# Stack stage: mix by head with 64 key rows, values copied from SBUF to SBUF, centred norms

## The chip, the cores and the metric
One core of a Trainium2 chip runs the whole program. The time is that of the device, from launch to end, in microseconds (us); three runs of the kernel before are given, and one execution that the profiler took.

## The reference
Eight sub-layers in a row work on x, of shape (2, 512, 128): an attention to 77 context rows by dynamic time warping, a quantised feed-forward, two attentions to the context with a mixture of experts between, a stack of six layers, an attention to latents and a second mixture of experts. Ahead of each a norm is taken. The change touches the norms and the stack. A layer of the stack, cut:

```
q, k, v = split(x @ Wqkv)                        # 16 heads of 64
q = rotary(l2norm(q)); k = rotary(l2norm(k))
bk, bv = [previous window of 32, own window]     # 64 keys for 32 queries
attn = softmax(where(mask, -big, 8 * q @ bk.T))
x = x + (attn @ bv) @ Wo
x = x + gelu-gated feed-forward(layernorm(shift(x)))
```
The norms compute `(x - mean) / sqrt(var + eps)`, some with `* gamma + beta`, some applied twice.

## The kernel before
x is kept with its 128 features in the partitions and its 1024 tokens along them, as two halves b of 512. TensorE (PE), VectorE (DVE), ScalarE (ACT), GpSimd (POOL) and SyncE (SP, which issues DMAs) each run a program of their own whose order is written out by hand; they meet only through semaphores.

**Norm.** `Norm.pe` multiplies each half with a matrix of 1/128 (the mean in every row, L174). `dve_centre` subtracts it on DVE (`xc`, L219), ACT squares (L208), PE sums the squares of each token (L186), ACT takes the root, DVE the reciprocal, PE spreads it over the partitions (L193), and DVE multiplies (L232, or L235 and with gamma and beta L237). With `plain` a second product goes to another tile (L241). It is used nine times: ahead of all sub-layers, and once within the third.

**Stack.** Twelve units u (six layers, two halves) of four tiles of 128 tokens make 48 tiles T. In round T of the loop PE projects tile T+2 (`pe_proj`, L1401: values in m = 0 and 1, then queries and keys), transposes r of T+1 (L1509), computes scores (L1530), transposed probabilities (L1582) and the mix (L1602) of T, and transposed output (L1626) and output product (L1650) of T-1. The feed-forward of unit u lies in the first two tiles of the unit after: its norm in t = 0, its products (L1740, L1742, L1765) in t = 1. t = 2 and 3 are plain tiles. PE may start projection m when the bank is free: the last two wait for `qk_used`, which DVE signals after its second table product (st_t, L1444).

Two heads e lie in one pair c: e = 0 in partitions 0 to 63, e = 1 in 64 to 127, each with 32 keys of the previous window (h = 0) and 32 of the own (h = 1). The scores are 64 products per tile, one for each pair, window w and head. The mix is 32 per tile: the stationary st_pT holds both heads in 128 rows and 32 queries, the moving st_vv 128 columns: for each head 64 columns, with zeros in the other head's rows. Each fp32 product makes two weight loads and two matmuls in the trace.

The values reach st_vv by way of DRAM: `sp_shift(T)` stores st_v (512 KB, L1343) when ACT has evacuated it, waits until mix T-2 is done, loads the last window of T-1 (only for t > 0), waits for the store, and loads four (256 KB) and three (192 KB) windows for each head (L1333). st_v and st_vv have two buffers. ACT overwrites st_v of tile T-2 once `v_stored` says that it is in DRAM (L1412). The loads of the next layer's weights are issued on SP behind tiles t = 3 to 6 of each layer (L1311 to L1323).

Of the kernel before, what the change touches and what calls it, by code (L numbers as in the profile page):

```python
# [78 lines left out]
def build(nc, io):  # L79
# [66 lines left out]
    class Norm:  # L146
# [3 lines left out]
        def __init__(self, tag, parts=(0, 1), chain=None):  # L150
            self.parts, self.chain = parts, chain or order
            self.mean_ready = sem(tag + "_mean_ready")
# [16 lines left out]
        PLAIN = (5, 4)  # L169

        def pe_mean(self, pe, b, src, src_ready, banks):
            if src_ready is not None:
                pe.wait_ge(src_ready, n("pe", src_ready))
            pe.matmul(PS[:, banks[b], :], const("mean"), src[:, b, :], start=True, stop=True)\  # L174
              .then_inc(self.mean_ready, 1)

        def pe(self, pe, src, src_ready, plain=False, banks=(6, 7), made=0):
# [4 lines left out]
            for b in self.parts:  # L182
                pe.wait_ge(self.squared, n("pe", self.squared))
                for j in range(self.BLOCKS):
                    at = self.BLOCKS * b + j
                    mm = pe.matmul(PS[:, banks[self.parts[0]], at:at + 1], sq[:, b, P * j:P * j + P],  # L186
                                   const("mean")[:, 0:1], start=True, stop=True)
# [15 lines left out]
        def act(self, act, twice=False, banks=(6, 7)):  # L203
# [6 lines left out]
            var = PS[:, banks[self.parts[0]], 0:B * self.BLOCKS]  # L210
# [10 lines left out]
        def dve(self, dve, src, dst, gamma=None, beta=None, twice=False, plain=None, banks=(6, 7), made=0):  # L221
            self.uses["dve"] = self.uses.get("dve", 0) + 1
            c = self.chain
            for b in self.parts[made:]:
                self.dve_centre(dve, b, src, banks)
# [3 lines left out]
            for b in self.parts:  # L229
# [18 lines left out]
    class Align:  # L248
# [151 lines left out]
        def ctx_pe(self, pe):  # L400
            pe.matmul(PS[:, 6, 0:B * KC], const("mean"), ctxT[:, :], start=True, stop=True).then_inc(norm.mean_ready, 1)
# [9 lines left out]
        def ctx_dve(self, dve):  # L411
            dve.wait_ge(norm.mean_ready, n("dve", norm.mean_ready))
            order.link(dve, dve.tensor_tensor(self.c0[:, :], ctxT[:, :], PS[:, 6, 0:B * KC], ALU.subtract))
            dve.tensor_tensor(self.c1[:, :], self.c0[:, :], self.c0[:, :], ALU.mult).then_inc(norm.squared, 1)

# [510 lines left out]
    class PairAttention:  # L926
# [41 lines left out]
        def act(self, act):  # L968
# [10 lines left out]
            norm.act(act)  # L979

        def dve(self, dve):
# [22 lines left out]
            norm.dve(dve, self.h2, xn, column("pa_ln2w"), column("pa_ln2b"))  # L1004
# [217 lines left out]
    class Stack:  # L1222
# [13 lines left out]
        def __init__(self):  # L1236
# [24 lines left out]
            self.v_out = dram("st_v_out", (4, P, INNER))  # L1261

            self.vv = s("vv", [P, 8, 2, INNER // 2])
# [15 lines left out]
             self.sub_done, self.exps, self.den_ready, self.rden_ready, self.v_stored, self.pv_done, self.on_ready,  # L1279
# [6 lines left out]
                "sub_done exps den_ready rden_ready v_stored pv_done on_ready wo_done xu_ready xf_ready centred lnsq "  # L1286
                "var std rstd spread ln_tmp ffn_in up gelu act_ready down down_added scaled masked").split()]
            self.vshift = [sem("st_vshift%d" % t) for t in range(4)]

# [38 lines left out]
        def v_load(self, sp, T, e, h, first, count, to, signal):  # L1328

            rows = slice(64 * e + WIN * h, 64 * e + WIN * h + WIN)  # L1330
            src = view(self.v_out, ((T % 4) * P + WIN * first) * INNER + 512 * e,
                       [[INNER, WIN], [WIN * INNER, count], [1, 512]])
            sp.dma_start(self.vv[rows, to:to + count, e, :], src).then_inc(self.vshift[signal], 16)  # L1333

        def sp_shift(self, sp, T):

            t = T % self.TILES
            at = 4 * (T % 2)
# [65 lines left out]
        def act_proj(self, act, T, m):  # L1404
# [189 lines left out]
        def pe_mix(self, pe, T):  # L1594
# [3 lines left out]
            pe.wait_ge(self.vshift[t], (u + 1) * (64 if t == 0 else 96))  # L1598
            for c in range(8):
                for w in range(4):  # L1600
                    g = slice(WIN * w, WIN * w + WIN)
                    mm = pe.matmul(PS[g, c // 4, P * (c % 4):P * (c % 4) + P], self.pT[:, c, g],  # L1602
                                   self.vv[:, 4 * (T % 2) + w, :, D2 * c:D2 * c + D2], start=(c % 4 == 0), stop=(c % 4 == 3),
                                   tile_position=(0, WIN * w), skip_group_check=True)
            mm.then_inc(self.pv_done, 1)

        def dve_out(self, dve, T):
            dve.wait_ge(self.pv_done, T + 1)
            dve.wait_ge(self.rden_ready, T + 1)
            if T > 0:  # L1610
                dve.wait_ge(self.o_turned, 2 * T)
            dve.tensor_tensor(self.on[:, :, :, :].rearrange("p (b c) e d -> p b (c e) d", b=2),
                              PS[:, 0:2, :].rearrange("p b (h d) -> p b h d", h=8),
                              self.rden[:, T % 2, :].rearrange("p (b h) -> p b h", b=2).unsqueeze(3)
# [281 lines left out]
        def dve(self, dve):  # L1896
# [7 lines left out]
            for T in range(-2, self.N + 3):  # L1904
# [34 lines left out]
                if end_of == self.LAST:  # L1939
                    norm.dve_centre(dve, 0, x, latents.NORM_BANKS)  # L1940
                    latents.ctx_dve(dve)

        def pool(self, pool):

            for k, what in enumerate((self.xs[64:P, :, 0:1], self.xf[64:P, 0:1], self.kT[:, :, 0:WIN],
                                      self.vv[:, 0:4, :, :], self.vv[:, 4:8, :, :])):
# [430 lines left out]
    def _(act):  # L2377
# [7 lines left out]
        norm.act(act, twice=True)  # L2385
# [7 lines left out]
        norm.act(act, twice=True, banks=latents.NORM_BANKS)  # L2393
        latents.act(act)
        norm.act(act, twice=True)
# [25 lines left out]
    def _(dve):  # L2421
        align.strips_dve(dve)
        dve.wait_ge(loaded, 16 * LOADS)
        norm.dve(dve, x, xn)
        align.dve(dve)
        norm.dve(dve, x, xn)
        quantised.dve(dve)
        norm.dve(dve, x, xn)
        attend1.dve(dve)
        norm.dve(dve, x, xn, column("pa_ln1w"), column("pa_ln1b"), twice=True, plain=pair.h0)  # L2430
        pair.dve(dve)
        experts1.dve(dve, pair.h2)
        norm.dve(dve, x, xn)
        attend2.dve(dve)
        norm.dve(dve, x, stack.y0)
        stack.dve(dve)
        norm.dve(dve, x, xn, column("la_g2"), column("la_b2"), twice=True,
                 banks=latents.NORM_BANKS, made=1)
        latents.dve(dve)
        norm.dve(dve, x, xn, column("m3_g"), column("m3_b"), twice=True, plain=h7)  # L2440
# [7 lines left out]
def spans(parts):  # L2448
    at, out = 0, {}
    for name, width in parts:  # L2450
# [6 lines left out]
                     ("hm", H), ("kidx", E), ("threehalves", 1), ("iota", S), ("blk8", P), ("centre", P)])  # L2457
# [113 lines left out]
```

## Time and profile before
| | us |
|---|---|
| median of 3 runs | 1928.72 (1924.58 to 1930.95) |
| the profiled execution | 1930.89 |
| its span, first to last instruction | 1929.1 |
| PE, DVE, ACT, POOL busy | 1614.8, 1254.7, 985.0, 760.8 |
| mean granted clock of TensorE | 0.92 of full speed |

Matmuls (PE) and weight loads (PEld) are shown as two engines. An arrow "<-DVE st_t L1444" behind a row names what ended the idle time before it; "issue" is idle time that nothing in the profile ended. A granted clock of 1.00 is TensorE's upper level, 2.4 GHz, and 0.50 its lower, 1.2 GHz.

### The profile page before, as it was taken

The numbers are of one execution on the slowest core, as the hardware profiler recorded it, in microseconds if no ns is written. First come the engines' busy times: TensorE is split into PE (matmuls) and PEld (weight loads), VectorE is DVE, ScalarE is ACT, GpSimd is POOL, SyncE is SP. The second block draws the span as 40 slices with busy tenths as digits, with TensorE's granted clock in tenths as the row PEclk, the third lists the DMA queues.
The fourth block names the chain that finished last, engine by engine and source line by source line (L and its number), as shares of the span: only waits on it lengthen the run. The fifth ranks groups of instructions, "written<-read, shape, count | busy, mean of one in ns | idle before, by whom it ended". The sixth has DMA issues, their size and how long they took to land. (4 is left out here: it accounts for less than half of the span.)

```text
span 1929.1 us, 42065 instructions
## 1 busy us (share of the span) xinstructions
PE 1614.8 (84%) x17121; PEld 1094.3 (57%) x17121; DVE 1254.7 (65%) x2359; ACT 985.0 (51%) x1853; POOL 760.8 (39%) x1082
## 2 busy tenths in 40 slices
PE   3005576998777899999999889999888999999999
PEld 1002264675645566666666666666664677666676
DVE  6847694213956788878887778888863666666311
ACT  1034133332335567657666556666654776777232
POOL 0000030100366576766776667776740333333000
PEclk6556698999979999999999999999998999999899
DMA  3000002010043433523533434433230000000111
GB/s 109 20 4 0 3 1 62 23 33 14 1 132 91 111 96 104 150 64 103 141 90 99 108 87 113 112 105 89 86 90 1 1 1 1 1 1 1 34 33 33
DMA packets 73801, 113.35 MB, mean 59 GB/s; under 512 B 16082, under 2 KB 36152, under 8 KB 73578
## 3 DMA queue, kind: packets, MB, share of 16 engines
q1 hardware_dynamic: 72794, 110.42, 20.7%
q8 instruction: 137, 2.24, 0.5%
q14 instruction: 54, 0.44, 0.1%
q10 hardware_dynamic: 816, 0.24, 0.1%
HBM read 83.96 MB, written 27.50 MB: 58 GB/s over the span
## 5 line engine op out<-in xcount | busy, mean ns | idle before, releaser
L1478 POOL TENSOR_TENSOR st_r<-st_r,st_t 128x512 f32<-128x512 f32 x192 | 243.8, 1274 | 212.0 <-DVE st_t L1444 212.0
L1401 PE MATMUL PS<-st_wqkv,st_xs 128*128 128x512 f32 x576 | 306.0, 616 | 12.2 <-DVE st_t L1444 7.7
L2252 POOL TENSOR_SCALAR la_p<-la_p,la_rden 128x589 f32<-128x589 f32 x64 | 112.9, 1763 | 232.9 <-DVE la_rden L2271 232.9
L1495 POOL TENSOR_TENSOR st_r<-st_r,st_gy 128x512 f32<-128x512 f32 x192 | 195.1, 1049 | 3.8
L1436 DVE TENSOR_TENSOR st_r<-PS,st_rot 128x512 f32<-128x512 f32 x192 | 129.2, 673 | 99.8 <-ACT st_sqh L1420 99.2
L1188 ACT ACTIVATE m_h<-PS 128x512 f32<-128x512 f32 x128 | 76.5, 598 | 143.0 <-PE PS L1120 143.0
L2265 DVE TENSOR_REDUCE la_nmx<-PS 128x1 f32<-128x589 f32 x128 | 92.7, 766 | 84.8 <-PE PS L2110 84.8
L1420 ACT ACTIVATE st_sqh<-PS 128x512 f32<-128x512 f32 x192 | 114.5, 597 | 57.6 <-PE PS L1401 57.0
L2217 ACT ACTIVATE la_p<-PS,la_nmx 128x589 f32<-128x589 f32 x128 | 95.2, 748 | 82.0 <-DVE la_nmx L2265 81.9
L1213 DVE SCALAR_TENSOR_TENSOR m_y<-PS,m_g,m_y 128x128 f32<-128x128 f32 x112 | 31.5, 344 | 161.0 <-PE PS L1129 161.0
L803 POOL MEMSET l_s<- 128x144 f32 x2 | 0.4, 220 | 331.7 <-DVE x L645 217.6
L1129 PEld LDWEIGHTS PS<-m_w,m_h 128*128 128x128 f32 x1024 | 121.4, 196 | 16.0 <-issue 16.0
L1444 DVE TENSOR_TENSOR st_t<-PS,st_rot 128x512 f32<-128x512 f32 x192 | 130.3, 679 | 0.0
L1449 DVE TENSOR_REDUCE st_ss<-st_sqh 128x8 f32<-128x512 f32 x192 | 129.5, 675 | 0.0
L1509 PEld LDWEIGHTS PS<-cst,st_r 128*128 128x128 f32 x768 | 91.2, 144 | 62.7 <-issue 44.4
L1129 PE MATMUL PS<-m_w,m_h 128*128 128x128 f32 x1024 | 121.6, 279 | 3.0 <-DVE m_y L1215 3.0
L1120 PE MATMUL PS<-xn,m_w 128*128 128x512 f32 x256 | 118.9, 610 | 0.0
L1650 PEld LDWEIGHTS PS<-st_oT,st_wo 128*128 128x128 f32 x768 | 94.4, 199 | 38.8 <-ACT st_oT L1635 29.1
L1509 PE MATMUL PS<-cst,st_r 128*128 128x128 f32 x768 | 111.1, 278 | 4.5 <-POOL st_r L1495 3.7
L1650 PE MATMUL PS<-st_oT,st_wo 128*128 128x128 f32 x768 | 102.1, 288 | 4.8 <-issue 2.7
L1401 PEld LDWEIGHTS PS<-st_wqkv,st_xs 128*128 128x128 f32 x576 | 89.7, 195 | 26.7 <-DVE st_t L1444 16.2
L1530 PE MATMUL PS<-st_kT,st_qT 64*32 64x64 f32 x6144 | 73.8, 226 | 36.1 <-issue 27.5
(312 smaller groups left out, 3483.2 us busy)
## 6 DMA issues: line engine op xcount, KB each, us to landing
st_v_out<-st_v SPq DMA_DIRECT2D x48, 512.0 KB, 2.6
st_vv<-st_v_out SPq DMA_DIRECT2D x96, 256.0 KB, 3.8
st_vv<-st_v_out SPq DMA_DIRECT2D x96, 192.0 KB, 4.4
st_wqkv<-in_st_wqkv SPq DMA_DIRECT2D x18, 512.0 KB, 5.8
m_w<-in_m_w SPq DMA_DIRECT2D x32, 256.0 KB, 3.2
st_vv<-st_v_out SPq DMA_DIRECT2D x72, 64.0 KB, 1.9
st_wo<-in_st_wo SPq DMA_DIRECT2D x6, 512.0 KB
st_w<-in_st_w SPq DMA_DIRECT2D x6, 341.0 KB
```

The source lines that it names most:

```text
L1120: pe.matmul(PS[:, c, :], self.w1[:, e % 2, P * c:P * c + P], xn[:, b, :], start=True, stop=True)\
L1129: mm = pe.matmul(PS[:, 4 + u % 2, P * j:P * j + P], self.h[:, u % 2, c, P * j:P * j + P], self.w2[:, e % 2, c, :], start=(c == 0), stop=(c ...
L1401: pe.matmul(PS[:, 2 + m % 2, :], self.xs[:, b, P * t:P * t + P], self.wqkv[:, l % 2, k, 512 * half:512 * half + 512], start=True, stop=Tru ...
L1420: act.activation(self.sqh[:, c % 2, :], ps, ACT.Square).then_inc(self.squares, 1)
L1436: dve.tensor_tensor(h3(self.r[:, t % 2, c, :]), h3(ps), self.rot[:, k, 0, t, :].unsqueeze(1) .broadcast_to([P, 8, D2]), ALU.mult)
L1444: dve.tensor_tensor(h4(self.t2[:, c % 2, :]), turned, self.rot[:, k, 1, t, :] .rearrange("p (s d) -> p s d", s=2).unsqueeze(1).broadcast_t ...
L1449: dve.tensor_reduce(self.ss[:, t % 2, 8 * c:8 * c + 8], h3(self.sqh[:, c % 2, :]), X, ALU.add)\
L1478: pool.tensor_tensor(r, r, self.t2[:, c % 2, :], ALU.add).then_inc(self.added, 1)
L1495: pool.tensor_tensor(r, r, y[:, 8 * c:8 * c + 8].unsqueeze(2).broadcast_to([P, 8, D2]), ALU.mult)\
L1509: mm = pe.transpose(PS[:, 4 + g % 2, P * j:P * j + P], self.r[:, T % 2, g, P * j:P * j + P], ident)
L1650: mm = pe.matmul(PS[:, 7, 0:P], self.wo[:, l % 2, c, :], self.oT[:, c, :], start=(c == 0), stop=(c == 7))
L2252: pool.tensor_scalar(self.p[:, v % 2, 0, :], self.p[:, v % 2, 0, :], self.rden[:, v % 4, 0:1], None, ALU.mult).then_inc(self.scaled0, 1)
```

## The change
**Mix.** 64 products per tile, one for each pair, window and head, with 64 stationary rows and 64 moving columns. st_vv loses its zeros: 512 columns per window instead of 1024. The result of head e goes to bank e of PSUM, and `dve_out` reads it in that order.

**Values.** No DRAM. `sp_shift(T)` waits for the evacuation and for mix T-2, and issues 14 DMAs from st_v to st_vv, of 32 rows by 2 KB each, preceded for t > 0 by two that cross from tile T-1. These two signal on semaphores of their own, `v_crossed`. ACT waits for the copies of T-2 and for the crossing copies of T-1 before it overwrites st_v, the mix for both kinds.

**Norms.** PE multiplies with `centre` (identity less 1/128), so the product is centred. ACT squares it from PSUM; DVE copies it to xc once it is squared. The variance goes to bank 5. With gamma, DVE does one scalar_tensor_tensor and ACT adds beta. `centre` moves into the first load of constants. At the stack's end `dve_keep` stands where `dve_centre` stood.

```diff
         def pe_mean(self, pe, b, src, src_ready, banks):
-            pe.matmul(PS[:, banks[b], :], const("mean"), src[:, b, :], start=True, stop=True)\
-              .then_inc(self.mean_ready, 1)
+            pe.matmul(PS[:, banks[b], :], const("centre"), src[:, b, :], start=True, stop=True)\
+              .then_inc(self.centred, 1)
...
-                act.activation(sq[:, b, :], xc[:, b, :], ACT.Square).then_inc(self.squared, 1)
+                act.activation(sq[:, b, :], PS[:, banks[b], :], ACT.Square).then_inc(self.squared, 1)
...
+            for b in self.parts if beta is not None else ():
+                act.wait_ge(self.scaled, n("act", self.scaled))
+                act.activation(dst[:, b, :], dst[:, b, :], ACT.Identity, bias=beta).then_inc(self.normed, 1)
-        def dve_centre(self, dve, b, src, banks):
-            dve.wait_ge(self.mean_ready, n("dve", self.mean_ready))
-            dve.tensor_tensor(xc[:, b, :], src[:, b, :], PS[:, banks[b], :], ALU.subtract).then_inc(self.centred, 1)
+        def dve_keep(self, dve, b, banks):
+            dve.wait_ge(self.squared, n("dve", self.squared))
+            dve.tensor_copy(xc[:, b, :], PS[:, banks[b], :])
...
-                    c.link(dve, dve.tensor_tensor(dst[:, b, :], xc[:, b, :], PS[:, banks[b], :],
-                                                  ALU.mult))
-                    dve.tensor_scalar(dst[:, b, :], dst[:, b, :], gamma, beta, ALU.mult, ALU.add)\
-                       .then_inc(self.normed, 1)
+                    dve.scalar_tensor_tensor(dst[:, b, :], xc[:, b, :], gamma, PS[:, banks[b], :], ALU.mult, ALU.mult)\
+                       .then_inc(self.scaled, 1)
...
+        def v_copy(self, sp, T, e, h, w, signal):
+            source = 4 * T + w - (1 - h)
+            rows = slice(64 * e + WIN * h, 64 * e + WIN * h + WIN)
+            block = slice(WIN * (source % 4), WIN * (source % 4) + WIN)
+            sp.dma_start(self.vv[rows, 4 * (T % 2) + w, :],
+                         self.v[block, source // 4 % 2, 512 * e:512 * e + 512]).then_inc(signal, 16)
...
         def sp_shift(self, sp, T):
             sp.wait_ge(self.v_evac, T * 2 + 2)
-            if T >= 4:
-                sp.wait_ge(self.pv_done, T - 3)
-            sp.dma_start(self.v_out[t], self.v[:, t % 2, :]).then_inc(self.v_stored, 16)
             if T >= 2:
                 sp.wait_ge(self.pv_done, T - 1)
             if t > 0:
                 for e in range(2):
-                    self.v_load(sp, T - 1, e, 0, 3, 1, at, t)
-            sp.wait_ge(self.v_stored, T * 16 + 16)
+                    self.v_copy(sp, T, e, 0, 0, self.v_crossed[T % 2])
             for e in range(2):
-                self.v_load(sp, T, e, 1, 0, 4, at, t)
-                self.v_load(sp, T, e, 0, 0, 3, at + 1, t)
+                for w in range(4):
+                    self.v_copy(sp, T, e, 1, w, self.vshift[t])
+                    if w:
+                        self.v_copy(sp, T, e, 0, w, self.vshift[t])
...
-                    act.wait_ge(self.v_stored, T * 16 - 16)
+                    act.wait_ge(self.vshift[(T - 2) % self.TILES], ((T - 2) // self.TILES + 1) * self.OWN)
+                    act.wait_ge(*self.crossed(T - 1))
...
             for c in range(8):
                 for w in range(4):
-                    mm = pe.matmul(PS[g, c // 4, P * (c % 4):P * (c % 4) + P], self.pT[:, c, g],
-                                   self.vv[:, 4 * (T % 2) + w, :, D2 * c:D2 * c + D2], start=(c % 4 == 0), stop=(c % 4 == 3),
-                                   tile_position=(0, WIN * w), skip_group_check=True)
+                    for e in range(2):
+                        keys = slice(64 * e, 64 * e + 64)
+                        mm = pe.matmul(PS[g, e, D2 * c:D2 * c + D2], self.pT[keys, c, g],
+                                       self.vv[keys, 4 * (T % 2) + w, D2 * c:D2 * c + D2], start=(c == 0), stop=(c == 7),
+                                       tile_position=(64 * e, WIN * w), skip_group_check=True)
...
                 if end_of == self.LAST:
-                    norm.dve_centre(dve, 0, x, latents.NORM_BANKS)
+                    norm.dve_keep(dve, 0, latents.NORM_BANKS)
                     latents.ctx_dve(dve)
```

## Rows read from the trace of the kernel before
**Rows 1.** Stretches: busy us (instructions) of PE, PEld, DVE, ACT, POOL; PEclk, DMA share, GB/s.
```profile
551.00:1452.00 901.00, 828.67 (x12452) 553.98 (x12452) 702.14 (x1083) 566.53 (x925) 597.19 (x984) 0.98 0.37 103
736.00:806.00 70.00, 68.26 (x1049) 45.49 (x1044) 58.61 (x92) 47.58 (x79) 48.38 (x82) 1.00 0.41 115
```

**Rows 2.** Timeline, PE (start us, us, engine, line): first parts of two mixes.
```profile
735.58 1.63 PE L1602 MATMUL PS<-st_vv,st_pT 128*32 128x128 f32 x52
805.55 1.72 PE L1602 MATMUL PS<-st_vv,st_pT 128*32 128x128 f32 x54
```

**Rows 3.** Waits of PE's matmuls in the stack: total us, times, longest.
```profile
PE PS L1530 <- issue: 27.5, 10, 4.4
PE PS L1626 <- issue: 6.1, 2, 3.4
...
PE PS L1740 <- DVE st_hid L1757: 3.8, 6, 0.6
...
PE PS L1650 <- issue: 2.7, 2, 2.1
```

**Rows 4.** Timeline, PE: one scores block, cut in two.
```profile
610.27 1.37 PE L1530 MATMUL PS<-st_kT,st_qT 64*32 64x64 f32 x116 [1.26 <-ACT PS L1545]
616.06 0.46 PE L1530 MATMUL PS<-st_kT,st_qT 64*32 64x64 f32 x12 [4.42 <-issue]
```

**Rows 5.** The page: busy time; the code queue; a DMA group (count, KB, landing).
```profile
PE 1614.8 (84%) x17121; PEld 1094.3 (57%) x17121; DVE 1254.7 (65%) x2359; ACT 985.0 (51%) x1853; POOL 760.8 (39%) x1082
...
q8 instruction: 137, 2.24, 0.5%
...
st_vv<-st_v_out SPq DMA_DIRECT2D x72, 64.0 KB, 1.9
```

**Rows 6.** Stretches (columns as rows 1): before and in that stall.
```profile
608.00:613.00 5.00, 2.38 (x122) 1.74 (x120) 4.67 (x9) 2.48 (x4) 2.71 (x3) 0.93 1.03 256
614.00:617.00 3.00, 0.94 (x13) 0.71 (x14) 0.40 (x1) 0.00 (x0) 2.30 (x10) 0.50 0.00 0
```

**Rows 7.** Timeline of a quiet plain tile: DVE, PE, ACT and SP.
```profile
919.82 0.69 DVE L1436 TENSOR_TENSOR st_r<-PS,st_rot 128x512 f32<-128x512 f32 x1 [1.21 <-ACT st_sqh L1420]
...
921.25 1.95 PE L1602 MATMUL PS<-st_vv,st_pT 128*32 128x128 f32 x64
923.14 0.66 PE L1509 MATMUL PS<-cst,st_r 128*128 128x128 f32 x4
...
927.23 1.12 PE L1401 MATMUL PS<-st_wqkv,st_xs 128*128 128x512 f32 x2 [0.40 <-DVE st_t L1444]
928.28 1.48 PE L1530 MATMUL PS<-st_kT,st_qT 64*32 64x64 f32 x128
928.39 0.60 ACT L1413 ACTIVATE st_v<-PS 128x512 f32<-128x512 f32 x1
929.69 0.66 PE L1626 MATMUL PS<-cst,st_on 128*128 128x128 f32 x4
...
934.62 0.69 DVE L1436 TENSOR_TENSOR st_r<-PS,st_rot 128x512 f32<-128x512 f32 x1 [1.20 <-ACT st_sqh L1420]
...
938.43 2.68 SPq L1333 DMA_DIRECT2D st_vv<-st_v_out  x6
```

**Rows 8.** SBUF to SBUF DMAs of the alignment: issue ns (min/median/max), busy share.
```profile
L311 SPq DMA_DIRECT2D al_skew<-al_dist x8: 774/775/955, 20.3 to 26.2; - x8
...
20.00:29.00 9.00, 2.96 (x15) 1.63 (x13) 7.70 (x13) 0.81 (x2) 0.00 (x0) 0.79 0.21 34
```

**Rows 9.** Norms: the second half ahead of the stack, and two operations by line.
```profile
541.80 0.69 DVE L219 TENSOR_TENSOR xc<-x,PS 128x512 f32<-128x512 f32 x1 [0.42 <-PE PS L174]
...
542.52 0.63 ACT L208 ACTIVATE sq<-xc 128x512 f32<-128x512 f32 x1 [0.48 <-DVE xc L219]
...
L237 DVE TENSOR_SCALAR xn<-xn,vec x8: 545/546/547, 301.4 to 1804.4; 128x512 f32<-128x512 f32 x8
...
L922 DVE SCALAR_TENSOR_TENSOR x<-PS,vec,x x4: 743/747/751, 287.8 to 539.8; 128x512 f32<-128x512 f32 x4
```

More of the change, by code:

```diff
@@ L146, in build, with __init__ @@
     class Norm:
-        def __init__(self, tag, parts=(0, 1), chain=None):
-            self.parts, self.chain = parts, chain or order
-            self.mean_ready = sem(tag + "_mean_ready")
+        def __init__(self, tag, parts=(0, 1)):
+            self.parts = parts
+            self.scaled = sem(tag + "_scaled")
             self.centred = sem(tag + "_centred")
@@ L185, in pe @@
                     at = self.BLOCKS * b + j
-                    mm = pe.matmul(PS[:, banks[self.parts[0]], at:at + 1], sq[:, b, P * j:P * j + P],
+                    mm = pe.matmul(PS[:, self.VAR, at:at + 1], sq[:, b, P * j:P * j + P],
                                    const("mean")[:, 0:1], start=True, stop=True)
@@ L201, in pe, with act @@
                 mm.then_inc(self.spread_ready, 1)
-        def act(self, act, twice=False, banks=(6, 7)):
+        def act(self, act, twice=False, beta=None, dst=None, banks=(6, 7)):
             self.uses["act"] = self.uses.get("act", 0) + 1
@@ L215, in act, with dve @@
                 act.activation(rstd[:, 0, :], var, ACT.Sqrt, bias=const("eps")).then_inc(self.std_ready, 1)
-        def dve_centre(self, dve, b, src, banks):
-            dve.wait_ge(self.mean_ready, n("dve", self.mean_ready))
-            dve.tensor_tensor(xc[:, b, :], src[:, b, :], PS[:, banks[b], :], ALU.subtract).then_inc(self.centred, 1)
-        def dve(self, dve, src, dst, gamma=None, beta=None, twice=False, plain=None, banks=(6, 7), made=0):
+            for b in self.parts if beta is not None else ():
[4 more added lines that the diff above has]
+            dve.tensor_copy(xc[:, b, :], PS[:, banks[b], :])
+        def dve(self, dve, dst, gamma=None, twice=False, plain=None, banks=(6, 7), made=0):
             self.uses["dve"] = self.uses.get("dve", 0) + 1
-            c = self.chain
             for b in self.parts[made:]:
-                self.dve_centre(dve, b, src, banks)
+                self.dve_keep(dve, b, banks)
             dve.wait_ge(self.std_ready, n("dve", self.std_ready))
@@ L400, in ctx_pe @@
         def ctx_pe(self, pe):
-            pe.matmul(PS[:, 6, 0:B * KC], const("mean"), ctxT[:, :], start=True, stop=True).then_inc(norm.mean_ready, 1)
+            pe.matmul(PS[:, 6, 0:B * KC], const("mean"), ctxT[:, :], start=True, stop=True).then_inc(self.prod_ready, 1)
             pe.wait_ge(norm.squared, n("pe", norm.squared))
@@ L411, in ctx_dve @@
         def ctx_dve(self, dve):
-            dve.wait_ge(norm.mean_ready, n("dve", norm.mean_ready))
+            dve.wait_ge(self.prod_ready, B + 1)
             order.link(dve, dve.tensor_tensor(self.c0[:, :], ctxT[:, :], PS[:, 6, 0:B * KC], ALU.subtract))
             dve.tensor_tensor(self.c1[:, :], self.c0[:, :], self.c0[:, :], ALU.mult).then_inc(norm.squared, 1)
+            n("dve", norm.squared)
         def ctx_out_dve(self, dve):
@@ L978, in act @@
                .then_inc(self.exps, 1)
-            norm.act(act)
+            norm.act(act, beta=column("pa_ln2b"), dst=xn)
         def dve(self, dve):
@@ L1003, in dve @@
             dve.wait_ge(self.h2_ready, 2)
-            norm.dve(dve, self.h2, xn, column("pa_ln2w"), column("pa_ln2b"))
+            norm.dve(dve, xn, column("pa_ln2w"))
     class Experts:
@@ L2384, in _ @@
         attend1.act(act)
-        norm.act(act, twice=True)
+        norm.act(act, twice=True, beta=column("pa_ln1b"), dst=xn)
         attend2.kv_act(act, 3)
@@ L2392, in _ @@
         stack.act(act)
-        norm.act(act, twice=True, banks=latents.NORM_BANKS)
+        norm.act(act, twice=True, beta=column("la_b2"), dst=xn, banks=latents.NORM_BANKS)
         latents.act(act)
-        norm.act(act, twice=True)
+        norm.act(act, twice=True, beta=column("m3_b"), dst=xn)
         experts3.act(act)
@@ L2423, in _ @@
         dve.wait_ge(loaded, 16 * LOADS)
-        norm.dve(dve, x, xn)
+        norm.dve(dve, xn)
         align.dve(dve)
-        norm.dve(dve, x, xn)
+        norm.dve(dve, xn)
         quantised.dve(dve)
-        norm.dve(dve, x, xn)
+        norm.dve(dve, xn)
         attend1.dve(dve)
-        norm.dve(dve, x, xn, column("pa_ln1w"), column("pa_ln1b"), twice=True, plain=pair.h0)
+        norm.dve(dve, xn, column("pa_ln1w"), twice=True, plain=pair.h0)
         pair.dve(dve)
         experts1.dve(dve, pair.h2)
-        norm.dve(dve, x, xn)
+        norm.dve(dve, xn)
         attend2.dve(dve)
-        norm.dve(dve, x, stack.y0)
+        norm.dve(dve, stack.y0)
         stack.dve(dve)
-        norm.dve(dve, x, xn, column("la_g2"), column("la_b2"), twice=True,
+        norm.dve(dve, xn, column("la_g2"), twice=True,
                  banks=latents.NORM_BANKS, made=1)
         latents.dve(dve)
-        norm.dve(dve, x, xn, column("m3_g"), column("m3_b"), twice=True, plain=h7)
+        norm.dve(dve, xn, column("m3_g"), twice=True, plain=h7)
         dve.wait_ge(norm.plain_ready, 4)
```

36 lines of the change are left out of this document (20 added, 16 removed).

## The prediction
> **What bounds the kernel now.** I read the busy time by stage first. The stack stage is 901 of the 1929.1 us. TensorE is busy for 92% of it, VectorE for 78%, and the mix lies in it 48 times [rows 1]. The starts of the mix give the period [rows 2]: 735.58 and 805.55 with three between, so four quiet tiles take 69.97 us. Twelve such fours would be 840 us; filling and emptying the pipeline takes part of the rest of the 901, and another part is lost within.
>
> The list of waits says where: TensorE stands for 27.5 + 6.1 + 2.7 = 36.3 us in 14 waits that no semaphore ends ("issue"), ten of them before the scores [rows 3]. In the order of time one is seen to cut a scores block in two: 116 matmuls, nothing for 4.42 us, then the last 12 [rows 4]. Nothing in the program separates the 116th from the 117th. What does is code. The instruction queue q8 moved 137 packets of 16 KB [rows 5]; TensorE's 2 x 17,121 matmuls and weight loads make 250 instructions for each, some more with its waits. And a stall goes with full DMA engines: from 608 to 613 their busy share was 1.03, from 614 it was 0.00, and TensorE went on at 616.06 [rows 4, 6]. The code block stood behind data packets, and once these were gone it took about 3 us to arrive and to take effect. Behind the stall TensorE's clock is at its lower level, 1.2 GHz (granted clock 0.50 in 614 to 617, rows 6).
>
> Then one quiet tile, to see what the mix is worth [rows 7]. From 919.82 VectorE works without a break past 927.17, where its table product lets TensorE start a projection, for which TensorE had waited 0.40 us. TensorE then works through scores, transposes, the output product and a projection; ScalarE squares it, and VectorE, idle for 1.20 us, goes on at 934.62. That loop of 14.80 us is the tile. The mix (921.25) lies beside its VectorE half, and the wait of 0.40 us behind the mix is slack of TensorE.
>
> **The mix.** Before: 64 matmul records from 921.25 to the next instruction at 923.14, 1.89 us. After: 64 products of 64 rows, 32 columns and 64 moving columns, in 128 records: in form, count and order the scores, 928.28 to 929.69, 1.41 us [rows 7]. 0.48 us less in 48 tiles is 23.0 us if all of it counted. In a plain tile it doesn't: TensorE comes 0.48 earlier to the projection for which it already waits 0.40. In the tile with the end of the feed-forward it waits for VectorE right after the mix too (L1740 behind st_hid, 0.6 us [rows 3]). Only in the tile with the norm, and in tiles that stalls have made TensorE's, some of it is kept. I take 4 us (12 norm tiles at 0.2, the rest from disturbed ones); ends 0 and 23. What a change of tile shape costs lies in these intervals, with neighbours of the full shape in either kernel.
>
> The Trainium skill (TensorEngine Tiling (Array Packing), section Instruction Overhead) says that a matmul costs some 60 cycles whatever its length, and that row tiling gives up to twice the speed. This case has a row for the very form, 1.41 and not 0.95 us, so the row is used; with 0.95 the upper end of the saving would be 45 us, an estimate by that page.
>
> **Code.** The mix doubles its instructions: 64 more matmuls and 64 more weight loads in each of 48 tiles, 6144, or 24 code blocks more. Today a tile holds one run that eats 256 instructions in 1.41 us (scores), and one of 128 in 1.89. After it holds two of 256 in 1.41. A block that lies inside such a run is used up before the next can come, and TensorE stands. So twice as many places can stall: 28 for today's 14. But the stalls will be shorter. Today's mean is 2.6 us because the loads of st_vv and of weights fill the DMA engines for some five us after a mix (share 1.03 at 608 to 613 [rows 6]). After, SP feeds that queue slowly (below), and the block comes when it is asked for: of the 3 us a part is covered by what TensorE still has, I take 1.2 us each, 34 us. Half of them lie around the mix, where TensorE has 0.40 + 0.48 us of slack: 14 x 0.88 = 12 us less, leaves 22. And fewer are long enough to bring the clock down. Against 36.3: 14 us gained, with 1 taken off for weight loads, 13. Ends: 28 stalls as long as today's, 73 us, a loss of 36; 14 of 1.2, 17, a gain of 19.
>
> **The copies of the values.** Removed per tile: the store of st_v (512 KB), the wait for it, and four to six loads (six in 2.68 us [rows 7], 0.45 each). Added: 14 copies, 16 in tiles with a predecessor, of 64 KB each, from SBUF to SBUF. SP took 0.775 us for one such DMA at the alignment [rows 8], against 0.45 for one from DRAM: 16 x 0.775 = 12.4 us per tile, ends 7.2 (at 0.45) and 15.3 (at 0.955, the longest there). With a weight load it is 12.9, under the plain tile's 14.8. So SP hides it. Queued behind are the weight loads of the next layer, some 10 us later; they have whole tiles to come. 32 packets per 0.775 us are 2 for each of 16 engines. Today SP puts the same 1024 KB (2 x 256, 2 x 192, 2 x 64) into the queue within 2.68 us [rows 7]: that is why the engines were full.
>
> The new wait is ScalarE's before it overwrites st_v: it needs the crossing copies, the first two that SP issues after the mix. Mix ends 923.14, SP issues at 923.27, two issues take 1.55, a landing 1.9 (the 64 KB load, rows 5): 926.7. ScalarE wants them at 928.39 [rows 7], 1.7 us later. Behind it queue the transposed output and the second value copy; they could bear another us, as the projection that needs the bank comes four us later. I cost it at nothing; were each landing 3 us longer, 1 us in 36 tiles, 36 us. The memset of st_vv on GpSimd halves; VectorE's own work ahead of the stack hides it: 0 (nothing lost if not).
>
> **The norms.** Nine of them. Today: product, VectorE centres (541.80, 0.69 us), ScalarE squares (542.52) [rows 9]. After: ScalarE reads the centred product from PSUM when VectorE would have, and the square is 0.72 us earlier. VectorE's copy to xc (under 0.7 each) lies beside the variance's 16 matmuls and the root. All nine stand between stages on the chain: 9 x 0.72 = 6.5. Four have a gamma: today 0.69 (a product as L219) + 0.546 (L237) per half, one after the other on VectorE; after 0.747 (the form of L922) and 0.63 on ScalarE (as its square) beside the next half [rows 9]. The first half comes 0.14 later, the second at 2.12 instead of 2.47, with the wait between dropped some 0.4 earlier; together 1.0. Costs: the first load of constants grows by 64 KB, 0.3 us at 256 GB/s [rows 6]. At the stack's end the copy must wait for ScalarE's square, which stands behind a gelu and a table load, and VectorE's last addition of the stack waits behind it; today there is idle time ahead of that addition: 0.2, at most 2. Sum 7.0; ends 3 and 11.
>
> **Sum.** On the profiled execution's 1930.89 (span 1929.1 and 1.8 around it): -7 -4 -13 = 1906.9. The median of the runs is 2.2 lower, so 1904.7: **1905 us**.
>
> **Rivals.**
> - *The whole of the mix counts.* For it: TensorE is busy for 97% of a quiet stretch (68.26 of 70 us, rows 1). Against: the 0.40 us wait and the loop above. 1928.7 -7 -23 -13 = 1886.
> - *The stalls stay what they are*, more but shorter in equal measure, or not of code at all; the mix brings 2. 1928.7 -7 -2 = 1920. The Trainium skill (Runtime: NRT & Kernel Launch, section Instruction fetch mechanics) leads here: it puts 256 instructions in a block of 16 KB, which the 137 packets agree with, but says that fetching is mostly hidden. The cut scores blocks speak against that.
> - *Slower: the code comes late.* Every block waits behind copies as today, and there are twice the short blocks. Place: inside scores and mix; price 36 us; it decides if a 2 KB packet between SBUF and SBUF takes over 0.39 us (two in 0.775), for then the engines are full all the time. Against: at the alignment such DMAs back to back gave a busy share of 0.21 [rows 8]. 1928.7 -7 -4 +36 = 1954.
> - *Slower: SP becomes the bound*, over (14.8 - 0.45) / 16 = 0.90 us per copy. At 1.1 us, 18.1 in the 24 plain tiles, 3.3 each: 79 us, 1984.
>
> **Chances.** Forecast 0.45 (own range 1896 to 1914), whole mix 0.13, stalls stay 0.22, code late 0.14, SP 0.06. Under 0.3% (5.8 us) a measurement can't tell from no change. Faster by more: 0.45 + 0.13 + two thirds of 0.22, 0.72. Within: 0.11. Slower: 0.17. The range leaves out the late code, most of SP and a tail of the first rival: 1884 to 1932.
>
> **What would show it.** Right: st_pT's matmuls as 128 records in 1.4 us; the projection's wait for st_t near 0.9 us in plain tiles, and the period of four quiet tiles at 69 to 70 us; DMA share never near 1 for 5 us outside weight loads; issue waits more in number, near or under 1.5 us; norm squares straight behind L174. Wrong: a quiet four under 68.5 us (mix counts), issue waits summing to over 40 us, SP's copies back to back into the next mix, or ScalarE idle before L1413 for a DMA.

## The result: slower by 0.6%, where 1.2% faster was forecast
| | median us (lowest to highest) | runs |
|---|---|---|
| before | 1929.01 (1918.31 to 1938.19) | 20 |
| after | 1941.58 (1924.46 to 1950.58) | 20 |

The ratio of after to before is 1.0062, 95% interval 1.0041 to 1.0082. In a later comparison it was 1.0038 (1.0012 to 1.0065). I had forecast 1905, with a range of 1884 to 1932: the time lies outside, on the side of the rival "the code comes late".

The profiled execution of after took 1928.86 us (span 1927.0), the low end of its runs; a second one, taken beside the last experiments, took 1943.39 (span 1941.6). Where they differ I give both. The page of the first, busy time and code queue:

```profile
span 1927.0 us, 48632 instructions
...
PE 1594.3 (83%) x20193; PEld 1077.1 (56%) x20193; DVE 1254.0 (65%) x2351; ACT 991.1 (51%) x1861; POOL 756.0 (39%) x1082
...
q8 instruction: 161, 2.64, 0.6%
```

Against [rows 5] there are 3072 more matmuls, as many more weight loads, and 161 code blocks for 137: the 24 more that I had counted. TensorE's busy time has fallen by 20 us. The mix itself became as quick as reckoned. The timeline of TensorE, mixes of some quiet tiles:

```profile
1041.62 1.49 PE L1618 MATMUL PS<-st_vv,st_pT 64*32 64x64 f32 x128
...
1061.64 1.49 PE L1618 MATMUL PS<-st_vv,st_pT 64*32 64x64 f32 x128
...
1076.80 1.48 PE L1618 MATMUL PS<-st_vv,st_pT 64*32 64x64 f32 x128
...
1267.31 1.49 PE L1618 MATMUL PS<-st_vv,st_pT 64*32 64x64 f32 x128
...
1318.30 1.48 PE L1618 MATMUL PS<-st_vv,st_pT 64*32 64x64 f32 x128
...
1335.91 1.33 PE L1618 MATMUL PS<-st_vv,st_pT 64*32 64x64 f32 x111
```

Tiles without a stall, against those of before: t = 1 took 20.02 us (1041.62 to 1061.64; 21.14 before), t = 2 15.16 (15.16), t = 3 15.87 to 16.03 (15.66). t = 0 took 17.61 once (1318.30 to 1335.91), but 18.2 to 18.5 in three others (18.01). Four quiet tiles are 68.6 us where four lie in a row (1267.31 to 1335.91), and 69.3 to 69.7 when added up with the other values of t = 0: 0.3 to 1.4 less than before [rows 2]. If tiles stayed quiet, the kernel would be faster. They don't. The waits of TensorE's matmuls by line (us in total, times, longest), first execution, and then the lines of the second:

```profile
PE PS L1542 <- issue: 31.1, 16, 2.8
...
PE PS L1618 <- issue: 15.2, 12, 1.7
...
PE PS L1642 <- issue: 3.8, 2, 2.1
```
```profile
PE PS L1542 <- issue: 32.5, 15, 2.9
PE PS L1618 <- issue: 17.0, 13, 1.8
PE PS L1642 <- issue: 3.7, 2, 2.5
PE PS L1521 <- issue: 2.1, 3, 1.4
PE PS L1666 <- issue: 1.2, 3, 0.5
```

Before, 14 such waits took 36.3 us and none lay in the mix [rows 3]. Now 31 to 34 take 51 to 56, and a dozen cut the mix. One plain tile (t = 3) shows both kinds. The timeline of TensorE:

```profile
921.92 1.28 PE L1618 MATMUL PS<-st_vv,st_pT 64*32 64x64 f32 x105
924.62 0.42 PE L1618 MATMUL PS<-st_vv,st_pT 64*32 64x64 f32 x23 [1.41 <-issue]
...
929.92 1.03 PE L1542 MATMUL PS<-st_kT,st_qT 64*32 64x64 f32 x81 [0.29 <-ACT PS L1557]
933.74 0.84 PE L1542 MATMUL PS<-st_kT,st_qT 64*32 64x64 f32 x47 [2.79 <-issue]
934.51 1.12 PE L1642 MATMUL PS<-cst,st_on 128*128 128x128 f32 x4
935.42 1.92 PE L1412 MATMUL PS<-st_wqkv,st_xs 128*128 128x512 f32 x2
```

The tile lasts 21.07 us instead of 16.0: 4.2 of standing still, and then matmuls at half speed (the projection of two takes 1.92 us, elsewhere 1.02). The stretches of this tile say what the DMA engines did (columns as in rows 1):

```profile
834.00:839.00 5.00, 4.29 (x22) 2.39 (x20) 4.97 (x9) 4.11 (x7) 2.58 (x3) 1.00 0.31 76
...
921.00:926.00 5.00, 3.59 (x140) 2.69 (x139) 4.96 (x8) 1.80 (x4) 5.00 (x6) 1.00 0.06 20
931.00:934.00 3.00, 0.26 (x29) 0.26 (x33) 0.80 (x2) 0.00 (x0) 2.20 (x8) 0.98 0.32 78
934.00:937.00 3.00, 3.00 (x49) 1.90 (x30) 2.34 (x2) 0.60 (x1) 2.53 (x8) 0.50 0.39 93
```

The first row is a quiet tile, behind its mix: a DMA share of 0.31, where before it was 1.03 [rows 6]. Around the stall in the mix the share is 0.06, in the stall of the scores 0.32. The engines are far from full, and TensorE stands all the same: what is left as the cause is a block used up before the next is there. In the 3 us before a stall the share was 0.02 to 0.04 in eight of eleven mixes, and 0.3 to 0.5 before the scores, where the copies were running. Behind the second stall the granted clock is 0.50, the lower level.

**Where the stalls begin.** I numbered TensorE's rows in the trace (matmuls, weight loads and semaphore waits) in order of time, from 0. Of the waits without a releaser above 0.5 us in the stack, all (14 of before, 29 of after) begin at a row whose number is 193 modulo 256: the edge of a code block, not a place of the program. And a packet of q8, which had taken 0.9 to 1.6 us, had ended 1.2 to 1.6 us before TensorE went on.

**An account of the stack** (from its first mix to its last), worked out from each trace: length, stalls at such edges, time at the lower clock level, and the rest, which is length less stalls less half of that time (half, as matmuls take twice as long at the lower level: 1.92 us against 1.02 above). The number counts short stalls too.

| kernel | length | stalls (number) | at half clock | rest |
|---|---|---|---|---|
| before | 858.7 | 36.3 (14) | 30.7 | 807.1 |
| after, first | 873.4 | 50.9 (31) | 41.0 | 802.0 |
| after, second | 881.8 | 55.9 (34) | 51.2 | 800.3 |
| n_only | 857.3 | 31.0 (13) | 38.6 | 807.0 |
| c_only | 838.7 | 16.9 (10) | 17.1 | 813.3 |
| nc | 846.3 | 19.8 (11) | 24.9 | 814.1 |
| m_only | 898.2 | 70.7 (34) | 75.1 | 790.0 |
| nc_split | 890.8 | 51.3 (34) | 52.2 | 813.4 |
| a_wide | 836.0 | 22.6 (15) | 13.7 | 806.6 |
| a_pad224 | 884.6 | 59.7 (38) | 44.4 | 802.7 |
| a_pad96 | 882.1 | 61.0 (38) | 34.1 | 804.0 |
| a_mid | 865.1 | 22.6 (16) | 13.7 | 835.7 |
| a_midp | 875.0 | 35.6 (29) | 14.4 | 832.2 |
| nc_mid | 850.0 | 13.3 (11) | 4.5 | 834.5 |

In the eleven profiles with the order of work unchanged the rest is 790 to 814, while the length ranges over 62 us. Some of the time at half clock lies within the stalls and is counted twice (5.0 us in before, 2.0 and 2.7 in after, 11.2 in m_only), which moves a rest by 6 us at most. How much slow clock goes with how much stall isn't fixed: 51.2 us with 55.9, but 34.1 with 61.0 (a_pad96).

### The profile page after: what moved, and what is told of

The parts are those of the page before. It is cut to its first block and busy times, and to the rows that moved or that the text cites. A ratio compares the mean times of both kernels' runs of the same rounds, so it can differ in the third digit from the quotient of the medians.

```text
span 1927.0 us, 48632 instructions
## 1 busy us (share of the span) xinstructions
PE 1594.3 (83%) x20193; PEld 1077.1 (56%) x20193; DVE 1254.0 (65%) x2351; ACT 991.1 (51%) x1861; POOL 756.0 (39%) x1082
## 5 line engine op out<-in xcount | busy, mean ns | idle before, releaser
L1666 PEld LDWEIGHTS PS<-st_oT,st_wo 128*128 128x128 f32 x768 | 99.3, 207 | 37.3 <-ACT st_oT L1651 28.2
L1542 PE MATMUL PS<-st_kT,st_qT 64*32 64x64 f32 x6144 | 82.7, 227 | 40.0 <-issue 31.1
L1542 PEld LDWEIGHTS PS<-st_kT,st_qT 64*32 64x32 f32 x6144 | 70.9, 106 | 73.7 <-issue 72.2
```

The costliest lines, as they stand in the source:

```text
L1542: mm = pe.matmul(PS[WIN * w:WIN * w + WIN, e, D2 * c:D2 * c + D2], self.qT[64 * e:64 * e + 64, c, WIN * w:WIN * w + WIN], self.kT[64 * e:6 ...
L1666: mm = pe.matmul(PS[:, 7, 0:P], self.wo[:, l % 2, c, :], self.oT[:, c, :], start=(c == 0), stop=(c == 7))
```

## The experiments
Eleven more kernels, and after once more, in 5 to 12 runs each. A ratio is to the kernel before, run on the same chip, and can differ a little from the ratio of the medians.

**The three parts, one at a time.** n_only has the new norms and the stack of before; c_only the new `sp_shift`, with st_vv's zeros and the 32-product mix kept; m_only the new mix, fed by way of DRAM.

```diff
# c_only, in the stack of after (with the mix of before)
-            sp.dma_start(self.vv[rows, 4 * (T % 2) + w, :],
+            sp.dma_start(self.vv[rows, 4 * (T % 2) + w, e, :],
# m_only, in the stack of before
-            sp.dma_start(self.vv[rows, to:to + count, e, :], src)
+            sp.dma_start(self.vv[rows, to:to + count, :], src)
```

n_only. Expected: 

> The kernel before with the new norms alone. If the norms do what was worked out, 7 us less than before (1922), and the stack as before: about 14 issue waits of TensorE, 36 us. If the loss sits in the norms (a wait of VectorE at the stack's end, or ScalarE's extra work), 1929 or more.

c_only. Expected: 

> The kernel before with the direct value copies alone; st_vv keeps its zeros and the mix its 32 products. By the theory that TensorE waits for code behind DMA packets, the issue waits shrink from 36 us, as the DMA engines are no longer full behind each mix: 1905 to 1920. By the rival that 16 small SBUF to SBUF copies per tile cost time (SP, or code late behind them), 1935 to 1945 with as many or longer issue waits.

m_only. Expected: 

> The kernel before with the mix by head alone (64 products, no zeros), values still by way of DRAM. By the theory that the doubled instructions stall for code: 25 to 30 issue waits, as long as today's (2 to 3 us), 1945 to 1965. By the rival that the copies are what costs, the mix alone gives 1915 to 1929.

| | median us | ratio (95%) |
|---|---|---|
| n_only | 1920.65 | 0.9954 (0.9923 to 0.9985) |
| c_only | 1909.77 | 0.9915 (0.9887 to 0.9943) |
| m_only | 1966.17 | 1.0207 (1.0178 to 1.0236) |

The median of before beside them was 1927.65: -7, -18 and +39 us. The waits of c_only, and then of m_only:

```profile
PE PS L1539 <- issue: 14.0, 8, 2.6
PE PS L1637 <- issue: 2.6, 2, 1.8
...
```
```profile
PE PS L1530 <- issue: 44.3, 17, 4.5
PE PS L1604 <- issue: 16.9, 13, 1.7
PE PS L1628 <- issue: 8.7, 2, 4.9
```

The loss is the mix's alone. m_only is the rival "the code comes late" as I had described it, full queue and twice the short blocks: 34 stalls of 70.7 us at the edges. In one of them the DMA engines are full and then TensorE stands at the lower clock:

```profile
600.00:605.00 5.00, 2.83 (x124) 1.93 (x122) 4.86 (x9) 2.82 (x5) 3.08 (x3) 0.98 1.04 236
605.00:608.00 3.00, 0.00 (x0) 0.00 (x0) 0.00 (x0) 0.00 (x0) 2.28 (x10) 0.50 0.31 117
```

In c_only, with the code of before and no burst of copies, stalls last 1.7 us each instead of 2.6, and four of 14 are gone.

Full engines make a stall longer, but it doesn't need them. TensorE's rows are the same, in the same order, in m_only and after, so the same edge can be read in both. At the edge ahead of which m_only's engines were full (600 to 605, above), it stalls 4.46 us and after 2.40; either has 12 matmuls cut off, as in [rows 4]. At an edge where m_only's engines moved nothing, it still stalls 2.45 us, against 2.72 in after. The timeline of m_only and its stretch, then the same edge in after:

```profile
1058.58 0.77 PE L1530 MATMUL PS<-st_kT,st_qT 64*32 64x64 f32 x39 [2.45 <-issue]
1056.00:1058.50 2.50, 0.13 (x15) 0.00 (x0) 0.86 (x2) 1.37 (x4) 1.85 (x6) 1.00 0.00 0
```
```profile
1031.42 0.65 PE L1542 MATMUL PS<-st_kT,st_qT 64*32 64x64 f32 x39 [2.72 <-issue]
```

**Norms and copies without the mix.** nc is after with the zeros and the 32-product mix of before.

Expected: 

> Norms and direct copies with the mix of before: the change without the doubled instructions. By the code theory the best of the four, 1900 to 1912. By the rival that the copies cost, 1930 or more.

Measured: 1905.16 us, ratio 0.9911 (0.9876 to 0.9946). It beats both kernels. To after's ratio of 1.0062 (1.0038) the mix by head adds 0.0151 (0.0127), or 24 to 29 us.

**Is it the number of instructions or the form of the mix?** The mix by head changes both: twice the records, and tiles of 64 rows into banks by head. nc_split has the number without the form, a_wide the form without the number.

```diff
# nc_split: nc, each product in two
-                    mm = pe.matmul(PS[g, c // 4, P * (c % 4):P * (c % 4) + P], self.pT[:, c, g],
-                                   self.vv[:, 4 * (T % 2) + w, :, D2 * c:D2 * c + D2], ...)
+                    for e in range(2):
+                        at = P * (c % 4) + D2 * e
+                        mm = pe.matmul(PS[g, c // 4, at:at + D2], self.pT[:, c, g],
+                                       self.vv[:, 4 * (T % 2) + w, e, D2 * c:D2 * c + D2], ...)
...
# a_wide: after, 128 moving columns
-            for c in range(8):
+            for c in range(0, 8, 2):
...
-                        mm = pe.matmul(PS[g, e, D2 * c:D2 * c + D2], self.pT[keys, c, g],
+                        mm = pe.matmul(PS[g, e, D2 * c:D2 * c + 2 * D2], self.pT[keys, c, g],
...
```

nc_split. Expected: 

> The kernel with the new norms and the direct copies, its values still with zeros beside them and its mix over all 128 rows, but each of the mix's 32 products cut into two of 64 moving columns: 64 products, 128 records, the count of the kernel after, without its head-by-head tiles. The uncut one was 1905 us (ratio to before 0.991). If the doubled count of instructions is what costs, through blocks of code that come late: stalls as in the kernel after (about 30 in the stack, some 45 to 50 us, against 17 to 20 uncut), time 1930 to 1945, ratio 1.00 to 1.01. If it is the form (tiles of 64 rows, banks by head), the time stays at 1900 to 1910.

a_wide. Expected: 

> The kernel after, with its mix by head over 64 key rows, but in 32 products of 128 moving columns instead of 64 of 64 (the second half of the columns gets the weights of the first head: another result, the same form of tile). It has the records of the mix before, 64. If the count of instructions costs: 1900 to 1912 us, ratio near 0.991, issue waits under 25 us in the stack. If the form costs: 1935 to 1945, ratio near 1.006.

Measured: nc_split 1949.02 us, 1.0111 (1.0091 to 1.0130); a_wide 1894.73 us, 0.9827 (0.9803 to 0.9852). The waits of nc_split (its mix is L1618, too) and of a_wide:

```profile
PE PS L1542 <- issue: 34.1, 16, 3.0
PE PS L1618 <- issue: 11.1, 13, 1.4
...
```
```profile
PE PS L1542 <- issue: 20.9, 13, 2.7
PE PS L1642 <- issue: 1.7, 2, 0.9
```

That decides it. With the old form and the doubled number the stalls are there, in the mix as well, and 0.020 of the ratio to nc, 39 us, are lost, more than expected; with the new form and the old number none is in the mix, and it is 0.0084, 16 us, under nc, also more than expected. (Its mix takes 1.16 us, so that some of the 16 is work saved.) It is the number. The mix of nc_split takes 0.6 us longer than that of after, 2.07 us, and its stalls are shorter, 11.1 us in 13 against 15.2 in 12 and 17.0 in 13: what TensorE still has to do covers a part.

**Does it matter where the edges fall?** Waits that are long fulfilled, in an idle time of TensorE's before the stack, push all later edges on.

```diff
# a_pad224, a_pad96 (96 waits): align.pe
             quantised.weights_pe(pe)
+            for _ in range(224):
+                pe.wait_ge(self.xsq, B)
             pe.wait_ge(self.walked, 3)
```

a_pad224. Expected: 

> The kernel after, and nothing else than 224 waits on a semaphore that has long reached its value, executed by TensorE in an idle time of some 50 us during the alignment. They move every later boundary between blocks of 256 instructions by 224 (that is, 32 the other way). In the kernel after every long stall begins at such a boundary, and it stalls where the boundary lies in the last 90 or so instructions of a run of 256 quick ones (scores, mix). Going through the after trace with its stalls taken out and 3.95 us from the entry of one block to the readiness of the next, I get 24 us of stalls unmoved (49 were measured), 15 for this shift. Theory of code: stalls fall to some 32 us, time 1920 to 1930, ratio near 0.998. If the place of code does not matter, 1941, ratio 1.006.

a_pad96. Expected: 

> The same with 96 waits. The same reckoning gives 29 us of stalls where it gives 24 unmoved. Theory of code: stalls near 60 us, time 1945 to 1958, ratio 1.009 to 1.015, and in any case 15 us or more above the version with 224. If the place of code does not matter, 1941, the same as with 224.

Measured: 1945.92 us, 1.0118 (1.0095 to 1.0142), and 1948.44 us, 1.0099 (1.0068 to 1.0131). My numbers missed, and the experiment isn't the one described: two waits went into one instruction, so that the edges moved by 112 and 48 (48744 and 48680 instructions on the pages, against 48632). For these shifts the same reckoning gives some 26 and 18 to 20 us of stalls, where it gives 19 to 24 unmoved, depending on which small gaps are taken out; the traces have 59.7 and 61.0, where unmoved ones have 50.9 and 55.9. It predicts neither the sums nor their order. What the two do show is that the stalls move with the edges: counted with the added rows, 35 waits above 0.5 us of each lie at 193 modulo 256 again, now 112 or 48 instructions earlier in the work.

The place of an edge tells whether it stalls. In the eleven profiles with the order of work unchanged, 418 edges lie in the first 140 rows of a run of 256 quick ones (scores, or the mix of 128 records), and none of them stalls. From row 205 of such a run on, 110 of 111 stall in the six profiles with the long mix (for 0.2 to 4.5 us), and 43 of 55 in the five with the short one. Between, it varies. Of 125 edges in a mix of 64 records, a run of 128 rows, none stalls. So the mix by head made places to stall out of places that had none. How much a given place costs I can't tell in advance.

**Are the stalls shorter where the run of quick instructions is broken?** a_mid moves four transposes into the middle of the scores and four into that of the mix; a_midp a projection into the scores; nc_mid is nc with the first of these. after_again is the kernel after, beside them.

```diff
# a_mid (nc_mid: the scores alone)
             for c in range(8):
+                if c == 4:
+                    between()        # scores: turn_o(T - 1, 0), mix: turn_r(T + 1, 0)
                 for w in range(4):
# a_midp: between() in the scores is pe_proj(T + 2, 0)
```

after_again. Expected: 

> The kernel after once more, beside the two kernels below that rearrange it, and for a second profile of it: the first profiled execution, 1929 us, was at the low end of its runs (median 1942). In the profiles of eight kernels so far the stack, from the first mix to the last, is 802 to 814 us and the sum of the stalls at boundaries of code blocks and half of the time at half clock. Expected 1941 again, ratio 1.006; stalls in the stack 50 to 62 us.

a_mid. Expected: 

> The kernel after with the same instructions, two of them moved: the four transposes of the first half of the output, until now ahead of the scores, stand between the scores of heads 7 and 8, and the four of the first query half, ahead of the mix, stand between the mix of heads 7 and 8. A run of 256 quick instructions becomes two of 128 with 8 slower ones between, and the last block takes 0.6 us longer to use up. If the stalls come because 256 instructions are used up before the next block is there, each is some 0.6 us shorter: 31 x 0.6 = 18 us of stalls and a third of the time at half clock, 1941 becomes 1912 to 1926. If the length of a stall is set by something else (a fixed cost of a boundary), 1938 to 1945. A loss is possible where the later transposes hold up ScalarE: up to 0.6 us in 24 plain tiles.

a_midp. Expected: 

> The kernel after with the first projection of the tile after next (0.9 to 1.0 us), until now ahead of the scores, between the scores of heads 7 and 8; the mix as it was. Theory of code: 18 stalls at the scores shorter by 0.9, 16 us and some clock; but the projection comes 0.7 us later to ScalarE and VectorE, which wait for it in the plain tiles' loop, up to 0.7 x 36 = 25 us lost. 1920 to 1950, stalls at the scores 31 us down to 15 to 20; that sum, not the time, is what tells. Rival: the sum stays at 31.

nc_mid. Expected: 

> The best legitimate kernel so far (new norms and direct copies, the mix of before, 1905 us, ratio 0.991), with the transposes of the first output half between the scores of heads 7 and 8. Theory of code: 10 stalls of the scores shorter by 0.6, 6 us and some clock: 1896 to 1903, ratio 0.985 to 0.990. Rival: 1905.

| | median us | ratio (95%) |
|---|---|---|
| after_again | 1938.39 | 1.0038 (1.0012 to 1.0065) |
| a_mid | 1927.78 | 1.0013 (0.9985 to 1.0042) |
| a_midp | 1939.25 | 1.0051 (1.0030 to 1.0072) |
| nc_mid | 1911.10 | 0.9917 (0.9887 to 0.9947) |

The waits of a_mid, and its timeline (TensorE) around a scores block:

```profile
PE PS L1544 <- issue: 18.9, 12, 2.3
...
PE PS L1622 <- issue: 0.6, 1, 0.6
```
```profile
842.91 1.13 PE L1412 MATMUL PS<-st_wqkv,st_xs 128*128 128x512 f32 x2 [1.05 <-DVE st_t L1456]
843.97 0.86 PE L1544 MATMUL PS<-st_kT,st_qT 64*32 64x64 f32 x64
844.76 0.66 PE L1646 MATMUL PS<-cst,st_on 128*128 128x128 f32 x4
845.34 0.86 PE L1544 MATMUL PS<-st_kT,st_qT 64*32 64x64 f32 x64
```

With the same instructions, 8 slow ones (0.6 us) between two times 128 quick ones cut the stalls from 55.9 to 22.6 us, more than the 18 expected; those of the mix (17.0) all but vanish (0.6), and the low clock goes from 51.2 us to 13.7. The time gains little, 11 us by the medians and 5 by the ratios, whose intervals overlap (expected were 15 to 29), as the rest of the stack is 35 us longer: what was moved is late for its reader, TensorE now waits 1.05 us instead of 0.54 for st_t, and a plain tile takes 15.6 us. (What these longer waits ahead of the scores add to the shorter stalls behind them isn't separated from the break itself.) a_midp shows the same for the scores alone (stalls before them from 32.5 to 18.3 us, nothing gained in time), and in nc, with few stalls to shorten, the move loses about what it brings (0.9917 against 0.9911; 0.985 to 0.990 was expected).

## Why the prediction was wrong
**Norms, -7 (3 to 11): right.** n_only: -7.0 us by the medians, 3 to 15 less by the interval of the ratio. In the timeline of after, around the norm ahead of the stack:

```profile
528.58 2.13 PE L175 MATMUL PS<-x,cst 128*128 128x512 f32 x4
...
529.64 0.60 ACT L209 ACTIVATE sq<-PS 128x512 f32<-128x512 f32 x1 [0.62 <-PE PS L175]
...
530.75 0.60 ACT L209 ACTIVATE sq<-PS 128x512 f32<-128x512 f32 x1 [0.52 <-PE PS L175]
531.38 0.69 DVE L224 COPY xc<-PS 128x512 f32<-128x512 f32 x1 [0.42 <-ACT sq L209]
```

The last square ends 2.77 us after the first product starts, before 3.52 (542.52 + 0.63 less 539.63): 0.75 per norm, reckoned 0.72. The copy lies beside the variance's matmuls.

**Copies cost nothing: right for SP and ScalarE; the sum of their gain came out by luck.** SP issues 14 in 9.96 us, 0.71 each (estimate 0.775), and a landing takes 2.0 us (1.9). ScalarE overwrites st_v without a wait for a DMA; what it waited for here was the projection:

```profile
833.92 9.96 SPq L1342 DMA_DIRECT2D st_vv<-st_v  x14
...
839.55 0.60 ACT L1425 ACTIVATE st_v<-PS 128x512 f32<-128x512 f32 x1 [0.46 <-PE PS L1412]
```

For the code of before without the burst, the step reckons 14 stalls of 1.2, 17 us; c_only has 10 of 1.7, 16.9 us. The product agrees, but neither the number nor the length does. Its stack is 20.0 us shorter: 19.4 of stalls and half of 13.6 us at the low clock, less a rest that is 6 longer, of which no run shows the cause.

**The mix, -4 (0 to 23): the record time was right** (1.41 us to the next instruction, 1.48 with the last end), and four quiet tiles are 0.3 to 1.4 us shorter, 4 to 16 us over twelve fours: the 4 reckoned or more, but not where I had put them. t = 2 keeps its 15.16, as argued (the 14.80 that I called the tile is one interval of VectorE; the mixes of plain tiles lay 15.16 and 15.66 apart). t = 3 loses 0.2 to 0.4. t = 0, where I counted on 0.2, ran from 0.4 shorter to 0.5 longer. t = 1, put at nothing, gains 1.1: I had read the wait for st_hid [rows 3] as slack there, where TensorE sets the pace.

**The failed step is "Code"**, its term for the doubled instructions of the mix. It put 28 stalls of 1.2 us, less 12 us covered by slack around the mix, 22 in all, against the 36.3 of before a gain of 13. Measured in the stack is a loss of 20 to 30: 15 to 20 of stalls and 5 to 10 of slow clock. The number was nearly right (31 to 34). Three things in it were not:
- *The length.* Of some 3 us for the arrival of a block I took all but 1.2 as covered. The mean is 1.6: 1.9 before the scores (31.1 / 16), 1.3 in the mix (15.2 / 12), with DMA engines far from full. The trace of before held a warning, a stall of 2.57 us without full engines:

```profile
1330.50 0.31 PE L1530 MATMUL PS<-st_kT,st_qT 64*32 64x64 f32 x5 [2.57 <-issue]
...
1325.00:1328.00 3.00, 2.53 (x128) 1.58 (x127) 2.93 (x6) 2.97 (x5) 1.37 (x2) 1.00 0.41 80
1327.00:1330.00 3.00, 0.93 (x90) 0.78 (x82) 1.63 (x4) 1.84 (x4) 2.25 (x5) 1.00 0.02 5
```

  In the same trace a late block's packet took 1.0 to 1.4 us and ended 1.2 to 1.6 us before TensorE resumed, together more than the 1.4 us of a quick run. When a block is asked for no trace shows, so what sets the exact length stays open, and also why it is longer before the scores than in the mix.
- *The cover.* Only t = 2 and 3 have the slack, 0.54 us (reckoned 0.88). In t = 1 there is none. One mix of such a tile, at 885.13, stalls for 1.21 us, and the tile takes 21.64, not 20.02: dearer than the stall.

```profile
885.13 1.43 PE L1618 MATMUL PS<-st_vv,st_pT 64*32 64x64 f32 x123
887.77 0.31 PE L1618 MATMUL PS<-st_vv,st_pT 64*32 64x64 f32 x5 [1.21 <-issue]
906.77 0.45 PE L1618 MATMUL PS<-st_vv,st_pT 64*32 64x64 f32 x31
```

- *The clock.* "Fewer are long enough to bring the clock down" was asserted without a row. The time at the lower level went from 30.7 to 41.0 and 51.2 us, which is 5 to 10 us more.

The sum with what was measured, second execution: stack +23.1 (stalls +19.6, clock +10.2, rest -6.8), norms and start -10.6 outside it: +12.5, the difference of the spans. Against my -17 in the stack. The rest lies within what quiet tiles give (-4 to -16). By the table the mix alone takes 17 off it (m_only) and the copies alone add 6; why, stays open.

The rival that won was given 0.14 because copies from SBUF wouldn't fill the DMA engines. They don't (0.31). The rival's own condition failed, and its outcome came all the same: I had tied the lateness of code to full queues, from one cut scores block [rows 4, 6], and never asked what a block costs without them. The Trainium skill (Runtime: NRT & Kernel Launch, section Instruction fetch mechanics) says that crossing a block of 16 KB is "mostly hidden". The block's size agrees with this case (edges every 256 rows). By number "mostly" does too: of 122 edges in the stack of after some 90 cost nothing. But the other 31 cost 51 us, and those late in a run of 256 quick rows all stalled (18 of 18 from row 205 on).

## What to carry to other kernels
Before cutting matmuls into more and smaller ones, count instructions per microsecond, and how long the run is: one in which TensorE uses up 256 of them in 1.4 to 2.1 us stopped nearly wherever a code block ended in its last 50, mostly for 1 to 3 us and often with a slow clock behind, while a mix of 128, with slower work on either side, never did; here 64 more matmuls and weight loads in 0.4 us less cost 24 to 29 us in 48 tiles. Number the engine's rows: if the waits without a releaser share a remainder modulo 256, it is code. Slow instructions in the middle of the run shorten the stalls, but pay only if they are free to move, which here they weren't; and transfers that fill the DMA engines just then should be spread, which brought 18 us here.

## What the runs showed of the hardware
- In the 14 profiles of 13 kernels the edges lay at one remainder, 193 modulo 256 of TensorE's rows, and so did all 310 waits of matmuls above 0.5 us in the stack that the profile puts down to "issue"; added instructions shift them exactly.
- In the first 140 rows of a run of 256 quick ones no edge of 418 stalled; from row 205 on 153 of 166 did; in a mix of 128 rows with slower work on either side none of 125.
- With a DMA share of 0.06 a block still comes 1.4 us late in a run of 256 instructions in 1.4 us, and with 0.00 in the stall it was 2.45 us late (m_only); behind a share of 1.03 to 1.04 it was 4.4 to 4.5 us.
- Products with 128 stationary rows and 64 moving columns took 2.07 us for 128 records (nc_split), with 64 rows 1.48.
- Two consecutive waits of TensorE on one semaphore made one instruction (224 gave 112, 96 gave 48).
